# Layer 0 feed-forward: rows normalised and scaled on ScalarE a tile ahead of VectorE's clip, and the power of the statistics taken in two parts

## What is computed

```python
x = x + L0_ffn(layernorm(x), w_gate, w_up, w_down)

def act_quant(x):                       # per token, 8 bits
    scale = 128 / clip(max(abs(x)), 1e-5)
    return clip(round(x * scale), -128, 127) / scale
def bitlinear(x, w):   return act_quant(x) @ weight_quant(w).T         # weights in {-1, 0, 1} times a scale
def h_bitlinear(x, w): return act_quant(fwht(x)) @ weight_quant(w).T   # fwht: Walsh-Hadamard over 1024
gate, up = bitlinear(x, w_gate), bitlinear(x, w_up)                    # 256 -> 1024
return h_bitlinear(silu(gate) * up, w_down)                            # 1024 -> 256
```

## Time and profile before

| what | us |
|---|---|
| three runs: median (lowest to highest) | 1629.64 (1629.09 to 1630.54) |
| the profiled execution | 1628.51 |
| its span, first to last instruction | 1626.7 |
| busy in the span: PE, DVE, ACT, POOL | 1352.0, 1071.2, 777.4, 631.9 |
| this stage, from the power's start to the last `add_to_x` | 273.2 to 454.6 |

### The profile page before, as it was taken

How to read it: one execution, slowest core, us unless ns; L and a number is a source line. 1 busy time by engine, 2 the same in 40 slices (tenths; PEclk the granted TensorE clock), 3 DMA queues, 4 the chain that set the end, 5 groups by cost and what they waited for, 6 DMA issues and landing times. The chain is left out here.

```text
span 1626.7 us, 29297 instructions
## 1 busy us (share of the span) xinstructions
PE 1352.0 (83%) x7976; PEld 845.5 (52%) x7992; DVE 1071.2 (66%) x2429; ACT 777.4 (48%) x2322; POOL 631.9 (39%) x649
## 2 busy tenths in 40 slices
PE   3899996566759969799997999978995999978993
PEld 2555553345534434476554666554663666654662
DVE  3898896788748855422664888875334888864224
ACT  2676773344540025432105888842442788833330
POOL 3112420777757523474002112112444665214661
PEclk9999997899979959999997999998998999998997
DMA  4231001400010022397501000141442210411224
GB/s 151 76 83 48 17 15 62 149 0 0 1 52 0 0 84 75 109 303 222 157 1 48 25 28 22 49 159 43 133 128 74 65 49 29 172 55 56 84 84 162
DMA packets 96447, 124.80 MB, mean 77 GB/s; under 512 B 11117, under 2 KB 76464, under 8 KB 96112
## 3 DMA queue, kind: packets, MB, share of 16 engines
q1 hardware_dynamic: 85392, 95.63, 18.5%
q0 software_dynamic: 10608, 28.07, 5.9%
q10 hardware_dynamic: 368, 0.16, 0.0%
HBM read 91.31 MB, written 33.43 MB: 77 GB/s over the span
## 5 line engine op out<-in xcount | busy, mean ns | idle before, releaser
L695 ACT ACTIVATE l0a_prob<-l0a_ps_s,l0a_neg_max 128x128 f32<-128x128 f32 x512 | 137.6, 398 | 67.7 <-DVE l0a_neg_max L553 60.0
L695 ACT ACTIVATE l2a_prob<-l2a_ps_s,l2a_neg_max 128x128 f32<-128x128 f32 x512 | 138.3, 399 | 26.7 <-DVE l2a_neg_max L553 21.7
L1135 ACT ACTIVATE l3a_prob<-l3a_ps_s,l3a_neg_max 128x256 f32<-128x256 f32 x256 | 104.3, 482 | 33.9 <-DVE l3a_neg_max L1050 32.3
L216 POOL TENSOR_TENSOR ln_rstd<-ln_var_eps,minus_half 128x16 f32<-128x16 f32 x7 | 20.5, 2922 | 233.5 <-POOLq L171 207.0
L553 DVE TENSOR_REDUCE l2a_neg_max<-l2a_ps_s 128x4 f32<-128x512 f32 x128 | 85.5, 683 | 19.1 <-PE l2a_ps_s L793 18.1
L501 POOL TENSOR_TENSOR l2a_k_head<-l2a_kT,head_of_row 128x512 f32<-128x512 f32 x32 | 32.9, 1047 | 161.7 <-DMA l2a_kT<-k_rows 161.7
L562 DVE COPY l0a_probT<-l0a_ps_t 128x512 f32<-128x512 f32 x128 | 84.4, 680 | 15.4 <-PE l0a_ps_t L805 15.2
L1050 DVE TENSOR_REDUCE l3a_neg_max<-l3a_ps_s 128x2 f32<-128x512 f32 x128 | 84.0, 679 | 14.2 <-PE l3a_ps_s L1186 13.0
L553 DVE TENSOR_REDUCE l0a_neg_max<-l0a_ps_s 128x4 f32<-128x512 f32 x128 | 85.2, 681 | 10.4 <-PE l0a_ps_s L793 9.6
L1748 PE MATMUL l1a_ps_y<-l1a_kv,l1a_tap 128*128 128x512 f32 x192 | 84.3, 602 | 3.7 <-POOL l1a_kv L1720 3.7
L501 POOL TENSOR_TENSOR l0a_k_head<-l0a_kT,head_of_row 128x512 f32<-128x512 f32 x30 | 30.8, 1047 | 145.6 <-DMA l0a_kT<-k_rows 145.6
(11 more groups left out here) (477 smaller groups left out, 3532.4 us busy)
## 6 DMA issues: line engine op xcount, KB each, us to landing
l1f_w_gu<-in_l1f_w_gu SPq DMA_DIRECT2D x32, 352.0 KB, 6.8
expert_results<-zeros SPq DMA_DIRECT2D x1, 8320.0 KB, 26.3
l1f_got<-expert_results SPq DMA_DIRECT2D x16, 512.0 KB, 3.9
expert_results<-l2f_y_sb SPq DMA_DIRECT2D x47, 128.0 KB, 1.7
l1f_w_d<-in_l1f_w_d SPq DMA_DIRECT2D x32, 176.0 KB
l2f_w_gu_all<-in_l2f_w_gu SPq DMA_DIRECT2D x1, 4096.0 KB, 15.2
l3f_w_gu_all<-in_l3f_w_gu SPq DMA_DIRECT2D x1, 4096.0 KB, 15.4
l3f_got<-expert_results SPq DMA_DIRECT2D x16, 256.0 KB, 5.0
```

What stands on the lines that cost most here:

```text
L695: last = act.activation(prob[4 * c + j][:, r * P:r * P + P], ps_s[j][:, r * P:r * P + P], ACT.Exp, bias=neg_max[:, j, r:r + 1])
L1135: last = act.activation(prob[4 * c + j][:, m * D:m * D + D], ps_s[j][:, m * D:m * D + D], ACT.Exp, bias=neg_max[:, j, m:m + 1])
```

## The change

`normalise` and the rounding multiply leave DVE. ACT does both as ACTIVATE Identity with a per-row scale and bias: `norm` (x * rstd + shift, with shift = -mean * rstd, which DVE makes in two small instructions) and `round_x` (xn * a_rec + magic, into a tile `xr` of its own). `quantise_x` becomes `measure_x` (maximum, scale, reciprocal, `deq`) and `clip_x`. `xn`, `a_max` and the loop's form change so that `norm` runs five tiles ahead, `measure_x` and `round_x` four, and `clip_x` three. POOL takes the power of the first 3 columns, then of the other 13. PE's and POOL's tile code is unchanged. The line numbers of the changed kernel differ.

```diff
...
+def over_x_pipe(eng, body):
+
+    body(0, 0)
+    body(1, 1)
+    with eng.Fori(1, B // 2 - 3) as i:
+        body(i * 2, 0)
+        body(i * 2 + 1, 1)
+    for t in range(B - 6, B):
+        body(t, t % 2)
+
+
...
+
+def rstd_in_parts(pool, core, done):
+
+    for part in (slice(0, FIRST), slice(FIRST, B)):
+        pool.tensor_tensor(core.rstd[:, part], core.var_eps[:, part], core.minus_half[:, part], ALU.pow).then_inc(done, 1)
 
 def normalise(dve, core, out, b):
@@ -1279,10 +1297,12 @@
         down_w = wq[2][:, :].rearrange("p (c f) -> p c f", c=NF)
         had = core.had
         magic = sb("magic", [P, 1])
-        xn = sb("xn", [P, D])
+        xn = [sb(f"xn{u}", [P, D]) for u in range(2)]
+        xr = sb("xr", [P, D])
+        shift = sb("shift", [P, B])
         xq = sb("xq", [P, D], BF16)
         xqT = [sb(f"xqT{u}", [P, KC, P], BF16) for u in range(2)]
-        a_max, a_rec = sb("a_max", [P, 1]), sb("a_rec", [P, 1])
+        a_max, a_rec = [sb(f"a_max{u}", [P, 1]) for u in range(2)], sb("a_rec", [P, 1])
         deq = [sb(f"deq{u}", [P, 2]) for u in range(2)]
         b_max, b_rec = sb("b_max", [P, 1]), sb("b_rec", [P, 1])
         b_deq = [sb(f"b_deq{u}", [P, 1]) for u in range(2)]
@@ -1308,7 +1328,8 @@
              "const_done", "xq_done", "deq_done", "xqT_put",
              "xqT_done", "gate_put", "up_put", "silu_done", "prod_done", "mixed_done", "mixT_put", "mixT_done",
              "had_put", "b_scale", "round_done", "hq_done", "hqT_put", "hqT_done", "y_put", "x_done"))
-        rstd_done = sem("rstd_done")
+        rstd_done, shift_done, normed, x_scaled, x_rounded = (sem(n) for n in (
+            "rstd_done", "shift_done", "normed", "x_scaled", "x_rounded"))
         zeroed = sem("zeroed")
         block = st.enter_context(nc.Block())
@@ -1320,7 +1341,7 @@
         @block.gpsimd
         def _(pool):
-            all_rstd(pool, core, rstd_done)
+            rstd_in_parts(pool, core, rstd_done)
             pool.memset(core.zeros[:, :], 0.0).then_inc(zeroed, 1)
             pool.memset(magic[:, :], MAGIC).then_inc(const_done, 1)
@@ -1341,25 +1362,25 @@
         @block.vector
         def _(dve):
-            def quantise_x(t, u):
-                dve.drain()
-                normalise(dve, core, xn[:, :], t)
-                dve.drain()
-                dve.tensor_reduce(a_max[:, :], xn[:, :], AX.X, ALU.max, apply_absolute_value=True)
-                dve.drain()
-                dve.tensor_scalar(a_max[:, :], a_max[:, :], 1e-5, 1.0 / 128, ALU.max, ALU.mult)
-                dve.drain()
-                dve.reciprocal(a_rec[:, :], a_max[:, :])
-                if after(t, 2):
-                    dve.wait_ge(silu_done, t - 1)
-                dve.tensor_scalar(deq[u][:, :], w_mean[:, 0:2], a_max[:, :], None, ALU.mult)\
+            def shifts(lo, hi):
+                dve.scalar_tensor_tensor(out=shift[:, lo:hi], in0=core.stats[:, lo:hi, 0], scalar=-1.0, in1=core.rstd[:, lo:hi],
+                                         op0=ALU.mult, op1=ALU.mult).then_inc(shift_done, 1)
+
+            def measure_x(t, u):
+                dve.wait_ge(normed, t + 1)
+                dve.tensor_reduce(a_max[u][:, :], xn[u][:, :], AX.X, ALU.max, apply_absolute_value=True)
+                dve.drain()
+                dve.tensor_scalar(a_max[u][:, :], a_max[u][:, :], 1e-5, 1.0 / 128, ALU.max, ALU.mult)
+                dve.drain()
+                dve.reciprocal(a_rec[:, :], a_max[u][:, :]).then_inc(x_scaled, 1)
+                dve.tensor_scalar(deq[u][:, :], w_mean[:, 0:2], a_max[u][:, :], None, ALU.mult)\
                    .then_inc(deq_done, 1)
-                dve.drain()
-                dve.tensor_scalar(xn[:, :], xn[:, :], a_rec[:, :], MAGIC, ALU.mult, ALU.add)
-                dve.drain()
+
+            def clip_x(t):
+                dve.wait_ge(x_rounded, t + 1)
                 if after(t, 1):
                     dve.wait_ge(xqT_put, t)
-                dve.tensor_scalar(xq[:, :], xn[:, :], MAGIC, 127.0, ALU.subtract, ALU.min).then_inc(xq_done, 1)
+                dve.tensor_scalar(xq[:, :], xr[:, :], MAGIC, 127.0, ALU.subtract, ALU.min).then_inc(xq_done, 1)
             def gate_times_up(t, u):
                 dve.wait_ge(silu_done, t + 1)
@@ -1393,27 +1414,47 @@
                 row_stats(dve, core, t)
             def tile(t, u):
-                if ahead(t, 3):
-                    quantise_x(t + 3, 1 - u)
                 if ahead(t, 2):
                     gate_times_up(t + 2, u)
                 scale_h(t, u)
+                if ahead(t, 3):
+                    clip_x(t + 3)
                 if after(t, 1):
                     add_to_x(t - 1, 1 - u)
+                if ahead(t, 4):
+                    measure_x(t + 4, u)
                 quantise_h(t)
             dve.wait_ge(rstd_done, 1)
-            quantise_x(0, 0)
-            quantise_x(1, 1)
+            shifts(0, FIRST)
+            measure_x(0, 0)
+            clip_x(0)
+            dve.wait_ge(rstd_done, 2)
+            shifts(FIRST, B)
+            measure_x(1, 1)
+            clip_x(1)
             gate_times_up(0, 0)
-            quantise_x(2, 0)
+            measure_x(2, 0)
+            clip_x(2)
             gate_times_up(1, 1)
-            over_long_pipe(dve, tile)
+            measure_x(3, 1)
+            over_x_pipe(dve, tile)
             add_to_x(B - 1, 1)
             finish_stats(dve, core)
         @block.scalar
         def _(act):
+            def norm(t, u):
+                act.activation(xn[u][:, :], core.xt(t), ACT.Identity, bias=shift[:, bass.ds(t, 1)],
+                               scale=core.rstd[:, bass.ds(t, 1)]).then_inc(normed, 1)
+
+            def round_x(t, u):
+                act.wait_ge(x_scaled, t + 1)
+                if after(t, 1):
+                    act.wait_ge(xq_done, t)
+                act.activation(xr[:, :], xn[u][:, :], ACT.Identity, bias=magic[:, :], scale=a_rec[:, :])\
+                    .then_inc(x_rounded, 1)
+
             def copy_xqT(t, u):
                 act.wait_ge(xqT_put, t + 1)
                 if after(t, 2):
@@ -1457,14 +1498,29 @@
                 if ahead(t, 3):
                     copy_xqT(t + 3, 1 - u)
                 round_h(t)
-
+                if ahead(t, 4):
+                    round_x(t + 4, u)
+                if ahead(t, 5):
+                    norm(t + 5, 1 - u)
+
+            act.wait_ge(shift_done, 1)
+            norm(0, 0)
+            norm(1, 1)
             act.wait_ge(const_done, 1)
+            round_x(0, 0)
+            round_x(1, 1)
             copy_xqT(0, 0)
+            norm(2, 0)
             copy_xqT(1, 1)
             silu(0, 0)
+            round_x(2, 0)
+            act.wait_ge(shift_done, 2)
+            norm(3, 1)
             copy_xqT(2, 0)
             silu(1, 1)
-            over_long_pipe(act, tile)
+            round_x(3, 1)
+            norm(4, 0)
+            over_x_pipe(act, tile)
             copy_hqT(B - 1, 0)
             copy_hqT(B - 1, 1)
```

More of the change, by code:

```diff
@@ L90 @@
 READY = 3
+FIRST = 3
 RING = 4
```

## The result

| | before | changed |
|---|---|---|
| median of six runs | 1629.91 | 1670.00 |
| lowest to highest | 1627.43 to 1638.44 | 1665.83 to 1683.28 |
| profiled execution | 1628.51 | 1683.28 |
| its span | 1626.7 | 1681.5 |
| this stage, power to power of the next stage | 183.9 | 223.2 |

The ratio is 1.025, with a 95% interval of 1.0209 to 1.0291: slower by 40 us. By the two profiles the stage is 39.4 us longer. The changed kernel's profiled execution is its slowest run, 13 us over the median.

What follows compares the result with a forecast made beforehand. DVE's own work was taken to bound the kernel at 10.04 us a tile. Ring +23.4, head -3.6 and clock +4.6 make +24.4 on 1628.51, 1652.9; with 1.1 for the median 1654.0 us, range 1641 to 1672.

Steps and rivals of the forecast that it cites:

- rival 1: Steady tiles: the ring of waits as summed sets the period; own range 1642 to 1667 us, chance 0.80.
- rival 2: PE in the ring: transposes and products behind the second gap are slow besides `down`; 1686 us, chance 0.11.
- What bounds the kernel: Steady tiles before the change: DVE's own work sets the period of 10.04 us; the other engines wait for it.
- The 8.2: POOL's period in us: 10.04 with 1.87 idle; would bound if moving work off DVE were all.
- DVE's wait for `down`: DVE ahead of `add_to_x`: now stands while clip, row copy and `down` finish, 2.0 us formerly under DVE's work.
- ACT's wait for `a_rec`: ACT ahead of `round_x`: waits for `measure_x`, done after `add_to_x`, holding back `norm` and `copy_mixedT`; about 2 us.
- The ring of 12.0 us: Clip to next clip through PE, DVE and ACT: 11.27 us without the clip, 12.0 with it, against 10.04.
- The clip at 0.75: DVE's clip in the ring: 0.29 us with POOL idle, 1.19 beside a butterfly; 0.75, the middle, taken.
- The head: Stage start: the power in two parts and earlier rows of tile 2 bring tile 1's start forward, -3.6 us.
- The clock: PE's `down` at the low clock in half of 11 periods: +4.6 us, bounds 0 and +9.1.
- my third rival: Steady tiles: `round_x` and `copy_xqT` never late, POOL bounds at 8.2 us; faster, 1606 us, chance 0.04.

Runs made afterwards that it cites:

- e9: The changed kernel run again with nothing altered, for a second profile; ratio 1.0271 to the kernel before.
- e3: Changed kernel with the clip ahead of gate_times_up on DVE and round_x with norm behind silu on ACT; ratio 0.9872 to the kernel before, 1615.5 us.
- e6: Changed kernel with the clip ahead of gate_times_up and measure_x ahead of add_to_x on DVE, ACT unaltered; ratio 0.9799 to the kernel before, 1626.9 us.
- e7: Changed kernel with PE computing the gate product twice and the second half of the transposes of hq five times; ratio 1.013 to the kernel before.
- e5: Kernel before with only the power split in two parts and DVE waiting for the second ahead of tile 3's rows; ratio 0.9997 to the kernel before.
- e1: Changed kernel with the clip of tile t+3 moved back ahead of gate_times_up on DVE; ratio 0.997 to the kernel before, 1629.2 us.
- e10: Changed kernel with clip ahead of gate_times_up, measure_x ahead of add_to_x, and magic set ahead of the powers; ratio 0.9842 to the kernel before, 1603.9 us.
- e4: Changed kernel with PE computing the gate product three times and the second half of the transposes of hq five times; ratio 1.0188 to the kernel before, 1661.4 us.

## Why the prediction was right or wrong

**The sign, the mechanism and the range were right, the size was short by 16 us** (1654 forecast, 1670.0 measured, 1672 the upper end). The range held by little: rival 1's own range ends at 1667, and only the 5 us added for rival 2 take in the result. By e9's ratio the same kernel would be at 1674 (an estimate, 1.0271 x 1629.9), outside it.

*What bounds the kernel.* DVE's own work set 10.04 us. With the work moved and both new waits removed, e3 and e6 run at 8.5 and 8.2, POOL's period. The 8.2 read from POOL's idle time was right: in e3 the butterflies wait for `prod` 1.1 us in 11 tiles.

*DVE's wait for `down`, ACT's wait for `a_rec`.* Both are in the trace, 11 times each, 28.1 and 27.4 us from tile 1 to 12. Removing the first gives 10.35, the second 11.32, both 8.52. Neither is the cause alone: they are links of one ring, and each move takes one of them out.

*The ring of 12.0 us.* Its links were summed from the trace of before; the periods of e7 at the full clock are 12.13 to 12.27. The mechanism is shown: both moves that break the ring were made, alone and together, and the ring's own length was measured.

*The clip at 0.75.* From `b_rec` to the clip's end are 0.19 to 1.13 us in the changed kernel, 0.64 in the mean of the 11 periods (0.86 in e9), so the middle was a fair choice.

*The head.* 3.6 us were forecast; 4.2 are there in the first profile (36.41 in place of 40.62 to tile 1) and 2.9 in the second (37.70). e5 gives the power's share: 1.6. In e5 a slow transform in the last tiles took as much back; that one follows from the other isn't shown.

*The clock.* This is the term of the sum that was mis-sized. I put it at 4.6 us: 0.83 for `down` in half of 11 periods, with 9.1 as its bound. Link by link, in the mean of the 11 periods and in us (the forecast's lengths are those at the full clock, ahead of the 4.6):

| link | forecast | changed | e9 | e7 |
|---|---|---|---|---|
| copied rows to the end of `down` | 1.18 | 1.56 | 1.25 | 1.54 |
| `copy_mixedT`'s end to the transform's end | 3.72 | 5.03 | 5.15 | 3.78 |

So what I priced came out as priced: `down` is slow in 5 of the 11 periods of the changed kernel and costs 4.1 us. What I left out of the sum is the second gap, ahead of `turn_mixed`. It was named, but priced only in a rival at 0.11. Behind it nine periods of the changed kernel lose 1.4 to 1.6 us and one 0.3, 14.4 in all, and 15.8 in e9: the earlier trace rows gives 1.03 and 1.11 to groups that take 1.82 and 1.91 above. Three periods (the 5th, 7th and 9th) lose behind both gaps and are the longest, 14.68, 14.42 and 14.38. The other links together are 1.5 under the ring's 131.5, which makes 148.6, as measured. The last three tiles take 26.92 against 24.0; 2.2 of that are again a slow `down` and a slow transform. In all the clock cost about 21 us in this stage, where 4.6 stand in the sum. My second rival, with both gaps slow in each period, gave 1686: too much, since `down` was slow in under half of them, and behind the second gap 1.4 to 1.6 were lost where it charged 2.5. The result lies between the two.

The rule of the Trainium skill in "TensorE: Matmul & The Clock Gate", section "HAM oscillation — how this bites in real kernels", that idle gaps bring the half-rate clock back each time, is borne out here in part. The page says it of waits for DMA, which are longer than the gaps here. At two gaps of 1.1 to 3.0 us per tile the granted clock is 0.78 to 0.84, and in e3 and e6, whose PE gaps ahead of the rows' transposes are about 0.7 us, it is 1.00. But not every gap here does it: in e9 `down` follows one of up to 3.0 us and is fast in ten of the eleven periods, and e1 has one of 2.3 us in each tile at a clock of 1.00 in nine of eleven. What I took from the rule was its effect on one group of matmuls.

*The rivals.* The Trainium skill's page "Perfetto Trace Analysis", section "Optimizing Scalar/DVE Operations", says that offloading from a saturated DVE may make sense. Taken as a rule that it gains, as in my third rival, that is right about the work, and wrong about this kernel as changed: the same offload is 0.984 of the kernel before in e10 and 1.025 in the change. The difference is the place of three calls in two hand-written orders.

What stays open: what sets behind which of the two gaps a given period loses the clock. e7 shows only that filling the second gap frees what follows it, and leaves the loss behind the first.

## What to carry to other kernels

When work leaves an engine, first read what it was hiding. Here gate_times_up and scale_h covered a path clip, PE, ACT, PE, DVE of 2.0 us, and the move of the clip laid it bare. An instruction given to an engine with idle time costs nothing only if its operand is ready when its turn comes: behind it stands all that follows in that engine's order, so put it where its producer is long done. And when a new wait makes PE stand, price its next matmuls at both levels of the clock, behind every gap and not only behind those that were slow before. The lower level is a bound, not a certainty: e1 has a gap of 2.3 us in each tile and nine of eleven periods at 1.00.

## What the runs showed of the hardware

The same matmuls per tile, with other engines' instructions in another order, ran at a granted clock of 1.00 (e3, e6), 0.97 (e1) and 0.78 to 0.84 (changed, e9). The clock is not set by the order alone: the kernel before had 0.95, and e5, with the same steady order and the same period, 0.91. Adding 4 to 8 redundant matmuls of 512 columns and 16 transposes per tile made the stage 7 to 8 us shorter (e4, e7). There may be a feedback in this, in which a longer period leaves PE idler, the clock falls and the period grows again; that is argued, and the runs show only that a period grows by 1.3 to 1.5 us where the clock is low.

A 128x256 ACTIVATE with per-row scale and bias took 0.58 to 0.60 us beside any DVE and POOL work, while DVE's multiply of the same rows took 0.35 with POOL idle and 1.25 with a butterfly running. DVE's small multiply for `deq` (128x2) took 0.21 us with POOL idle and up to 1.25 in the changed kernel when it started under a butterfly. It then lasted until that butterfly's end, as these rows of the changed kernel show (346.21 and 346.24), while the reciprocals of 128x1 took 0.15 to 0.17 throughout. It stands in no link of the ring that I summed:

```profile
344.95 1.26 POOL L1358 TENSOR_TENSOR l0f_mixed<-l0f_prod 128x512 f32<-128x512 f32 x1
...
345.34 0.90 DVE L1376 TENSOR_SCALAR l0f_deq<-w_mean,l0f_a_max 128x2 f32<-128x2 f32 x1
```
